# GNN stack on one core: three edge passes on plain tiles of 128 edges, with tables of tile-bucket pairs made on the chip

## What is computed

```python
edge_index = jnp.stack([src, dst])
# layer 0: messages of edges, summed at dst
m = jnp.concatenate([h[src], edge_attr_3], axis=1)
h_N = segment_sum(relu(m @ W1.T + b1), dst)          # then relu([h, h_N] @ W2.T), L2 norm
# layer 1: eight relations, summed at src
xt = einsum('ni,rio->rno', h, weight)
out = segment_sum(xt[edge_type, dst], src)           # then relu(out + bias)
# layer 2: attention with 8 heads, softmax over the edges at dst, summed at dst, then batch norm
# layer 3: w = dinv_sqrt[src] * dinv_sqrt[dst]
h = segment_sum(w[:, None] * h[dst], src)            # then h @ W + b, leaky relu
```

## Time and profile before

| | us |
|---|---|
| median of 3 runs | 5837.55 |
| lowest and highest | 5836.89, 5838.79 |
| the profiled execution | 5834.2 |
| its span | 5832.5 |

### The profile page before, as it was taken

One profiled execution on the slowest core, in us unless ns is written; L12 is line 12 of the kernel. 1 busy time (PEld: TensorE's weight loads), 2 busy tenths in 40 slices (PEclk: granted clock), 3 DMA queues, 4 the chain that ended last, 5 costly groups with the idle time before them and its releaser, 6 DMA issues. The chain is left out here.

```text
span 5832.5 us, 109209 instructions
## 1 busy us (share of the span) xinstructions
PE 4215.9 (72%) x13046; PEld 2391.6 (41%) x13047; DVE 3005.1 (52%) x8724; ACT 2211.5 (38%) x6436; POOL 4037.7 (69%) x4157
## 2 busy tenths in 40 slices
PE   4505777777764990798999856777777558898998
PEld 2303444444452440333333335666666323333335
DVE  8316666666642330433333357777777853333335
ACT  0203333333441110443433345666666344333444
POOL 2766777777777777777777717777777257777773
PEclk8756777776777995655555578888888755555557
DMA  1203333333302440444444424444444134444443
GB/s 53 66 25 85 101 101 101 101 101 101 84 3 61 154 148 16 106 108 108 108 108 109 108 69 102 109 110 109 109 109 109 49 108 108 108 108 109 108 108 99
DMA packets 762446, 552.76 MB, mean 95 GB/s; under 512 B 569128, under 2 KB 654847, under 8 KB 762106
## 3 DMA queue, kind: packets, MB, share of 16 engines
q0 software_dynamic: 184832, 443.09, 26.7%
q1 hardware_dynamic: 576888, 106.39, 9.1%
q10 hardware_dynamic: 640, 2.40, 0.1%
HBM read 467.71 MB, written 83.62 MB: 95 GB/s over the span
## 5 line engine op out<-in xcount | busy, mean ns | idle before, releaser
L921 PE MATMUL psS_plain_src<-got_plain_src,hot_plain_src 128*128 128x257 f32 x3328 | 1853.1, 670 | 446.3 <-ACT hot_plain_src L848 237.7
L921 PEld LDWEIGHTS psS_plain_src<-got_plain_src,hot_plain_src 128*128 128x128 f32 x3328 | 786.0, 293 | 1513.3 <-DVE sums L718 859.4
L718 DVE TENSOR_TENSOR sums<-sums,psS_plain_src 128x257 f32 x1664 | 706.1, 424 | 1256.7 <-PE psS_plain_src L921 1175.6
L668 POOL DMA_INDIRECT got_edge_mlp_dst<-dram_ptab,recs_edge_mlp_dst x832 | 856.0, 1029 | 284.1 <-ACT msg_edge_mlp_dst L874 111.0
L843 ACT ACTIVATE gap_plain_src<-iota,rel_plain_src 128x128 f32<-128x128 f32 x1664 | 531.3, 390 | 1358.3 <-DVE rel_plain_src L732 1355.9
L503 POOL DMA_INDIRECT dram_rec_src<-rec_src x784 | 764.9, 976 | 327.2 <-issue 243.6
L668 POOL DMA_INDIRECT got_attend_dst<-dram_gtab,recs_attend_dst x832 | 814.3, 979 | 254.5 <-issue 168.7
L668 POOL DMA_INDIRECT got_plain_src<-dram_htab,recs_plain_src x832 | 786.6, 945 | 254.2 <-issue 136.2
L668 POOL DMA_INDIRECT got_plain_src<-dram_xtab,recs_plain_src x832 | 786.6, 945 | 254.2 <-issue 151.5
L921 PE MATMUL psS_edge_mlp_dst<-msg_edge_mlp_dst,hot_edge_mlp_dst 128*128 128x256 f32 x1664 | 700.8, 568 | 178.4 <-DVE sage_sums L718 140.6
L921 PE MATMUL psS_attend_dst<-msg_attend_dst,hot_attend_dst 128*128 128x264 f32 x1664 | 605.8, 450 | 30.0 <-DVE sums L718 20.7
(11 more groups left out here) (289 smaller groups left out, 4111.8 us busy)
## 6 DMA issues: line engine op xcount, KB each, us to landing
dram_xtab<-out_tab SPq DMA_DIRECT2D x48, 1024.0 KB
recs_plain_src<-dram_rec_src SPq DMA_DIRECT2D x1664, 4.0 KB
recs_edge_mlp_dst<-dram_rec_dst SPq DMA_DIRECT2D x832, 4.0 KB
got_edge_mlp_dst<-dram_ptab,recs_edge_mlp_dst POOLq DMA_INDIRECT x832
got_plain_src<-dram_xtab,recs_plain_src POOLq DMA_INDIRECT x832
recs_attend_dst<-dram_rec_dst SPq DMA_DIRECT2D x832, 4.0 KB
got_attend_dst<-dram_gtab,recs_attend_dst POOLq DMA_INDIRECT x832
got_plain_src<-dram_htab,recs_plain_src POOLq DMA_INDIRECT x832
```

The source lines that it names most:

```text
L668: nc.gpsimd.indirect_dma_start(got[:, u, 0:w], None, table, bass.IndirectOffsetOnAxis(rec_i[:, u, index_word:index_word + 1], 0)).then_inc ...
L718: nc.vector.tensor_tensor(here, here, psS[t[1] % banks][:, 0:cols], ALU.add).then_inc(added, 1)
L921: nc.tensor.matmul(psS[t[1] % banks][:, 0:cols], hot[:, t[1], :], rows(t), start=True, stop=True).then_inc(sums, 1)
```

## The change

The second and fourth pass, and the first, no longer go over tiles that begin inside buckets. They gather **plain tiles**, the 784 blocks of 128 records, in a ring of their own. What the sums go over are **pairs** of a plain tile and a bucket of which it holds edges: a tile that lies across a bucket's end is in two pairs, and the sum of each pair takes the tile's rows with a mask for its own bucket. There are again at most 829 pairs, rounded up to 832. The third pass (`attend`) and the `max` pass keep their tiles.

Where a pair finds its bucket's place, its tile's offset, its slot among the 16 gathered tiles, and how many tiles must have landed, and where a tile finds how many pairs must be done before its slot is free, stands in tables. A new stage `pair_stage`, between the list stage of dst and the first pass, makes them for both directions: per direction eight products on PE and some thirty instructions on DVE (`PairTables`); `list_stage` only keeps the counts, and for dst the tile tables of the third pass. `CUTS` becomes 2, 4, 7, 2, 12, 22 rounds of scatters: two run beside `pair_stage`, two fewer beside `table_stage` 1.

The new `pair_pass` takes the place of `edge_pass` in three passes:

```diff
-                stage(nc, edge_pass, c, "dst", c.ptab, D, 0, "edge_mlp")
-                stage(nc, sage_update, c, of_src, cut[2], cut[3])
-            stage(nc, table_stage, c, 1, of_src, cut[3], rounds)
+            stage(nc, pair_stage, c, of_src, cut[2], cut[3])
+                stage(nc, pair_pass, c, "dst", c.ptab, D, 0, "edge_mlp")
+                stage(nc, sage_update, c, of_src, cut[3], cut[4])
+            stage(nc, table_stage, c, 1, of_src, cut[4], rounds)
...
-        stage(nc, edge_pass, c, "src", c.xtab, D, 0, "plain")
+        stage(nc, pair_pass, c, "src", c.xtab, D, 0, "plain")
...
-        stage(nc, edge_pass, c, "src", c.htab, D, 2, "plain")
+        stage(nc, pair_pass, c, "src", c.htab, D, 2, "plain")
```

```diff
+    tiles, pairs, shared = Ring(sh.COLS, U), Ring(sh.NT, U), Ring(sh.NT // share, U // share)
...
+                        sp.wait_ge(used, pairs_of.of(u))
+                        gate.step()
+                    sp.dma_start(tile_rec[:, u, :], rec_d[bass.ds(P * (tiles.count(t) - 1), P), :]).then_inc(tile_in[u], 16)
+                if (t := tiles.at(i, u, AHEAD)) is not None:
+                    sp.wait_ge(row_in[t[1]], 16 * (t[0] + 1))
+                    sp.sem_inc(landed, 1)
```

POOL, per plain tile; the wait for the slot is gone from POOL, and in the plain mode only a column of ones is filled in at the start, not the whole of `got`:

```diff
+                nc.gpsimd.memset(got[:, :, D:D + 1], 1.0).then_inc(start, 1)
...
+                pool.wait_ge(tile_in[u], 16 * (t[0] + 1))
+                gate.step()
+                nc.gpsimd.indirect_dma_start(got[:, u, 0:width], None, table,
```

ACT loads the records of each pair's window for the masks, eight pairs ahead. It makes no masks in these passes. DVE makes them in all three, one instruction for each pair, four in a row:

```diff
-                nc.vector.tensor_tensor(hot[:, u:u + 4, :], iota[:, :].unsqueeze(1).to_broadcast([P, 4, P]),
-                                        rel[:, u // 4 % 2, :].unsqueeze(2).to_broadcast([P, 4, P]), ALU.is_equal).then_inc(hots, 1)
+                for k in range(4):
+                    last = nc.vector.tensor_scalar(hot[:, u + k, :], c.iota[:, :], rel[:, u // 4 % 2, k:k + 1], None, ALU.is_equal)
...
+                    act.dma_start(rec[:, t[1], :], rec_d[bass.ds(offs.of(u), P), :]).then_inc(rec_in[t[1]], 16)
```

PE (plain) and DVE (`edge_mlp`) read the slot of a pair's rows and, for every second pair, the number of landed tiles to wait for, from registers:

```diff
+                        if not u % share:
+                            pe.wait_ge(landed, needs.of(u // share))
+                        wait_count(pe, added, pairs.count(t, bank_back(t)))
+                        nc.tensor.matmul(psS[t[1] % banks][:, 0:cols], hot[:, t[1], :], flat[:, bass.ds(slots.of(u), cols)],
```

More of the change, by code:

```diff
@@ L28 @@
 SLOPE = 0.2
-CUTS = 0.04, 0.12, 0.27, 0.52
+CUTS = 0.04, 0.12, 0.265, 0.30, 0.55
 U = 16
@@ L39 @@
 NODE_LAG = 4
+PAIR_MODE = {"dst": "edge_mlp", "src": "plain"}
+GOT_LAG = {"edge_mlp": 4, "plain": 0}
+SHARE = {"edge_mlp": 2, "plain": 2}
+AHEAD = 6
+EARLY = 8
 AWAY = 131072.0
@@ L114, in load @@
         there = [(u, t) for u in range(self.ring.size) if (t := self.ring.at(i, u, self.back)) is not None]
+        if not there:
+            return
         first, n = self.ring.count(there[0][1]) - 1, len(there)
@@ L117, in load @@
             self.values[0:1, bass.ds(first + self.ahead, n)], engines=[self.eng.engine], min_val=0, max_val=self.max_val,
-            skip_runtime_bounds_check_because="the lists hold at most NB buckets' places, and offsets up to EP - P")
+            skip_runtime_bounds_check_because="the lists hold at most NB buckets' places, offsets up to EP - P and counts of tiles and pairs")
         self.held = {u: v for (u, _), v in zip(there, held)}
     def of(self, u):
-        return self.held[u]
+        if not self.least:
+            return self.held[u]
+        self.eng.reg_alu(self.floor, self.held[u], self.least, ALU.max)
+        return self.floor
 class Gate:
@@ L162, in constants @@
     c.rank_of = sb("rank_of", [P, P], BF16)
+    c.before, c.upto = sb("before", [P, P], F32), sb("upto", [P, P], F32)
     c.x = sb("x_sb", [P, sh.NB, D], F32)
@@ L227, in list_stage @@
     rec, key, begins = edges.rec, edges.key, edges.begins
-    base_f, (place_i, ahead), (off_i, _) = c.tiles[kind]
+    nb = c.counts[kind]
     own = sh.E - (P - 1) * COLS
@@ L526, in edge_pass @@
     NT = sh.NT
-    base_f, place_i, off_i = c.tiles[kind]
-    if mode == "attend":
-        place_i = c.late
-    rec_d = c.rec_dst if kind == "dst" else c.rec_src
+    base_f, off_i = c.tile_base, c.tile_off
+    rec_d = c.rec_dst
     ring = Ring(NT, U)
@@ L533, in edge_pass @@
     nm = f"{mode}_{index_word}_{kind}"
-    cols = {"plain": D + 1, "edge_mlp": D, "attend": AW, "max": 0}[mode]
+    cols = {"attend": AW, "max": 0}[mode]
     with ExitStack() as st:
@@ L544, in edge_pass @@
         rels = sem("rels")
-        hot_on_act = mode in ("plain", "attend")
+        hot_on_act = mode == "attend"
         gap = sb("gap", [P, 2, 4, P], F32) if hot_on_act else None
@@ L660, in step @@
                 t = ring.at(i, u)
-                free = msgs if mode in ("edge_mlp", "attend") else sums
+                free = msgs if mode == "attend" else sums
                 if (old := ring.at(i, u, U)) is not None:
@@ L742, in one_hot @@
                                         rel[:, u // 4 % 2, :].unsqueeze(2).to_broadcast([P, 4, P]), ALU.is_equal).then_inc(hots, 1)
[L744 to L760 removed]
+            if mode == "attend":
                 def step(i, u):
@@ new lines, in pair_stage, with _ @@
+def pair_stage(nc, c, edges, first, end):
+    sh = c.sh
+    with ExitStack() as st:
+        tile_no = st.enter_context(nc.sbuf_tensor("tile_no_pairs", [P, sh.NT], F32))
+        ps = [st.enter_context(nc.psum_tensor(f"ps{k}_pairs", [P, 512], F32)) for k in range(7)]
+        numbered = nc.alloc_semaphore("numbered_pairs")
+        of_dst, of_src = PairTables(nc, c, "dst", st, (tile_no, ps)), PairTables(nc, c, "src", st, (tile_no, ps))
+        scatter = Scatter(nc, c, edges, first, end)
+        block = st.enter_context(nc.Block())
+        @block.gpsimd
+        def _(pool):
+            nc.gpsimd.iota(tile_no[:, :], pattern=[[1, sh.NT]], base=0, channel_multiplier=0,
+                           allow_small_or_imprecise_dtypes=True).then_inc(numbered, 1)
+            scatter.run(pool)
+        @block.tensor
+        def _(pe):
+            of_dst.tensor(pe, None)
+            of_src.tensor(pe, of_dst)
+        @block.vector
+        def _(dve):
+            dve.wait_ge(numbered, 1)
+            of_dst.dve(dve)
+            of_src.dve(dve)
```

535 lines of the change are left out of this document (362 added, 173 removed).

## The result

The changed kernel takes 5759.59 us (median of 4 runs, 5756.39 to 5761.06) where the kernel before takes 5838.17 (4 runs, 5836.89 to 5838.9): ratio 0.9862, 95% interval 0.985 to 0.9874, so 78.6 us less. The forecast was 217.6 us less (5620 us). The profiled execution has a span of 5757.0 us against 5832.5 and a granted clock of 0.755 against 0.701. (In the diff shown above, the lines of the wide mask stand as removed; they still stand in `edge_pass`, and `pair_pass` has the four narrow ones.)

A forecast was written before the change was run, and what follows sets the result against it. POOL issuing its gathers was taken to bound each pass. From the profiled 5834.2 us, -109.4 - 52.9 - 52.9 - 1.4 - 1.3 = -217.9 gave 5616.3, forecast as a median of 5620 us, range 5580 to 5715.

The forecast's parts named there:

- The second and fourth pass: Each falls from 1039.9 us to 987 us, -52.9, as POOL issues 784 gathers instead of 832.
- the first rival: Masks on DVE block POOL's gathers outright in the three changed passes: 1146 us each, time about 6085; chance 0.05.
- the third rival: PE bounds the second and fourth pass at 1.27 us a pair: 1057 us each, time 5760; chance 0.06.
- the fourth: SP's hand-over stretches POOL's gather spacing to 1.33 us; only the first pass gains, time 5766; chance 0.06.
- The mask term: First pass: each wide mask on DVE costs a gather about 0.34 us, 208 x 0.336 = 70 us.
- Tables and stages: Source list stage -8.4 us, destination list stage -1.1, new stage +48.6, last table stage -40.4: net -1.3.
- the sum of DVE's round: First pass: DVE's adds, masks, subtractions, waits and table reads take 17.7 to 19.6 us per 16 pairs.
- 4 small subtractions and the wait for the four edge products after each (4 x 0.4): Part of DVE's work per 16 pairs in the first pass, put at 0.4 us for each of four.
- ACT's share: First pass: ACT's message, load, copies and table read take 1.03 of 1.19 us a pair, so hidden.
- the second rival: DVE bounds the first pass at 1.25 us a pair: 1040 us, time 5660; chance 0.14.
- the signs that the prediction asked for: Changed profile: gathers 1.25 us apart, mean near 0.95; DVE waiting for landed rows; second pass about 110 us earlier.
- the forecast is wrong if ... POOL waits more than its 0.30 us: Failure sign: POOL's idle time before gathers exceeds 0.30 us, or gathers come in a second, long kind.

The follow-up runs named there:

- experiment 4: Changed kernel with the first pass as before: 5728.53 us; then with four narrow masks replacing that pass's wide one: 5660.48 us, 68.1 less.
- experiment 1: Changed kernel with PE issuing the first pass's edge product ahead of the next group's transpose instead of behind it: 5675.02 us.
- experiment 2: Changed kernel without ACT's read of the record offset table in the first pass, loads issued from a constant place: 5731.98 us.
- experiment 9: Changed kernel without ACT's record loads in the first pass after the first sixteen, table read kept: 5674.79 us.
- experiment 8: Changed kernel with the first pass's edge product issued in two pieces: 5669.17 us; a whole kernel also with two table reads a round: 5621.54 us.
- experiment 6: Changed kernel with the first pass's edge product issued first and DVE's read of the sums' places left out: 5597.26 us.

## Why the prediction was wrong

**The second and fourth pass: right.** 784 gathers at 1.254 us; 983 and 984 us where 987 were forecast. The narrow masks cost the gathers 3 ns (948 against 945) where 0.035 x 208 = 7 us were allowed. By the rule of the Trainium skill (SBUF - State Buffer, "Who interferes with whom") that stood behind the first rival, each burst would have blocked POOL if its compares ran in a two-port mode, and no run shows in which mode they ran; these 784 gathers per pass, beside 186 us of mask instructions on DVE, show 2.5 us in all. PE kept up at a mean granted clock of 0.72, so the third rival's price of 1.27 us a pair did not show, and the gathers' idle time stayed at 0.308 us each, which rules out the fourth.

**The mask term: right.** 70 us for 208 wide masks were read from two rows; experiment 4 measured 68.1.

**Tables and stages: right within 6 us.** The first pass starts 33.5 us later, not 39.1.

**The first pass: the step that failed is the sum of DVE's round**, "Sum 17.7 to 19.6 us a round", measured 22.2. Term by term: 32 adds by 0.33 = 10.6, as forecast. Masks 4 x 0.8 = 3.2, the upper end of 2.2 to 3.2. Three table reads 3.7 (2.31 + 1.41 us over a group without them) and the turn of the loop 0.4, together 4.1, the upper end of 3.3 to 4.2. The mis-sized term is "4 small subtractions and the wait for the four edge products after each (4 x 0.4)": 1.6 forecast, 3 x 1.20 + 0.34 = 3.9 measured. The 0.4 was no row's: before the change that wait lay under the wait for gathered rows, and nothing showed what it is when the rows are there. It is a chain across three queues: ACT's message, ACT's record load, `spread`, PE's transpose, the product, DVE. The prediction looked at ACT's share (1.03 of 1.19 us, "hidden, with little to spare") where its place in this chain counted. Without the order of PE's queue each wait is 0.5 us shorter (experiment 1), without ACT's table read 0.2 (experiment 2), without ACT's loads 0.5 (experiment 9); they overlap and do not add up.

These terms sum to 21.9 us; 0.3 of the 22.2 is left. A term that was not in the sum at all may be part of it: the low clock after the reads. In the changed kernel it is small. Groups directly behind the reads take 4.80 us where they lie wholly in it and 4.81 where they do not, for there DVE waits for the edge product anyway; the next ones take 4.63 us at the full clock (9 of them) and 4.91 where the low clock reaches into them (15; two more lie wholly in it, at 5.54), some 0.2 us a round. It begins to matter once the waits are gone (experiment 8).

With 22.2 us a round the mechanism of the second rival ("DVE bounds the first pass", 1.25 us a pair, 1040 us, 5660) is what happened, at 1.39 us a pair; both ends of the forecast's own DVE sum lay under the measured value, so the range (to 5715) couldn't hold it. That 5760 is also the figure of the third and fourth rival is chance.

**The tails** (12.5 + 5.1 + 4.1 us) were not forecast. After the last gather of the first pass DVE still has 20 sums to add, for 18.0 us, where it had 7, for 5.6 us; with DVE's round shortened (experiment 6) it is 15, for 11.6. That accounts for the 12.5; the two smaller ones were not looked into.

Of the signs that the prediction asked for, these held: 784 gathers with a mean of 0.95 us and few above 1.1 (none in the timelines), idle time before POOL named by SP's loads or none, PE in the plain passes with waits, the first pass some 40 us late (33.5). These failed: gathers 1.25 us apart in the first pass, DVE still waiting for landed rows there, the second pass 110 us earlier (it starts 29.6 later). Its own sentence "the forecast is wrong if ... POOL waits more than its 0.30 us" came true in the first pass (424.0 us of idle time before 784 gathers).

## What to carry to other kernels

When a change takes away the wait that an engine's time was hidden under, sum that engine's round anew and take each wait in it as a chain of queue places, not as shares of busy time: here loads of 0.34 us on a queue with room to spare went with 85 us of a pass (experiment 9), since they stood ahead of a copy that PE and DVE wait for. Count the reads of tables into registers as work (a read of 16 words delayed the next add by 1.4 us here), put few words of them on the engine that binds, and look what its stall does to the others. Where two suspects each bring the same gain alone, run both together: the 162 us for two edits of 85 told that they were terms of one series. Where four come out at one value, as here, doubt that each has been priced.

## What the runs showed of the hardware

- A read of 8, 16 and 32 table words into registers took DVE 0.60, 1.10 and 2.10 us, and no row counts it as busy; in the first pass of the changed kernel the reads of 16 words took 1.32, and 1.10 again when one of the three reads was gone. The Trainium skill (DMA: Bandwidth & Descriptors, "Latency and other measured facts") gives a floor of about 600 ns for such a load. The 0.60 us for 8 words agrees with it; one-word reads of `wide` took 0.30 us on ACT and 0.32 on DVE, under that floor, and the measurement decides. What a word adds, 0.06 us, the runs show.
- Four compares of 128 columns with a scalar, back to back, held DVE 0.8 us, and the gathers of such a pass were 3 ns longer on average (948 against 945); one two-input compare of 512 columns held DVE 0.6 us (0.69 long) and cost a gather 0.33 us. The slower way for DVE is the better one beside POOL; form and width were changed together.
- In experiment 8 a stall of DVE for its reads (1004.5 to 1009.3 us) left PE busy for 2.6 us in six, and the granted clock was then 0.50 instead of 1.00 for about ten us; it fell so 51 times in 52 rounds.
